# Rows scattered by rank, column-quarter loads turned by VectorE, and a new order of the shared chunks, in a gated two-layer kernel

## The chip, the cores and the metric

The kernel runs on one core of a Trainium2 chip. The metric is the time of one execution on the device in microseconds. TensorE is called PE here (its weight loads PEld), VectorE DVE, ScalarE ACT, GpSimd POOL and SyncE SP, as in the profile.

## What is computed

2048 tokens of 512 features. Layer 1: a layer norm without weights, then one of four gated units chosen by the token's id (the weights of all three products of a unit are the same 512 x 512 matrix), times a tanh gate, added to x. Layer 2: a layer norm, then a mixture of 16 experts of inner width 352, two per token and at most 256 places each, plus one shared gated unit of the same width that all tokens pass, times a second tanh gate, added.

```python
x = x + tanh(g_xattn[0]) * xattn(layernorm(x), token_ids, ctx, ctx, ctx)
x = x + tanh(g_ffn[0]) * ffn(layernorm(x), ...)
# ffn, cut:
scores = sqrt(softplus(xt @ gate_w.T)); _, idx = top_k(scores + gate_b, 2)
buf = zeros((16, 256, 512)).at[e, posc].add(x_pairs)      # dispatch by rank in expert
h = silu(buf @ W1.T) * (buf @ W3.T); out = h @ W2.T       # per expert, width 352
shared = (silu(xt @ Ws1.T) * (xt @ Ws3.T)) @ Ws2.T
return y + shared
```

All of it is float32. Matrix products are made of three products of a high part and a low part of each operand (`product`, L1441): ACT copies the high part out, DVE subtracts it to get the low part, and PE multiplies high by high, high by low and low by high.

## The kernel before, in words

Each engine has its own program in one block; the order of the work is written out by hand, and semaphores (`wait_ge`, `then_inc`) tie the programs together. There is no planner.

**Stage 1** (`step(t, par, known)` on each engine, 19 tiles `t` of 128 rows). Tokens are sorted by their unit, and each unit's group is filled up to whole tiles, so there are NT = 19 tiles for 16 tiles' worth of tokens. POOL gathers a tile's rows of x twice (`gather_xa` for the norm, `gather_xb` for the residual), PE transposes them and multiplies, DVE adds the residual (L1038), ACT writes the normalised rows into the right half of `xh_sb` (L687), and two things leave: POOL scatters both halves, 4 KB a row, to `out` by token (`scatter`, L470), and SP writes the right half, in tile order, to a DRAM tensor `padded` (L405). `xh_sb` has two buffers; DVE's residual of tile t waits until both writes of tile t-2 have landed (L1035, L1036).

**The shared unit.** `rank_gather(j)` on POOL (L481) gathers 128 rows of `padded`, skipping the fill, so that 16 row tiles `j` of ranked tokens come about; four make a block, block b = j // 4. Each row tile lies in `row_tile(j)` (L212), is transposed by PE in four 128 x 128 pieces (`transpose4`, L1447) into a PSUM bank `row_bank(j)`, copied to `bl[b]` by ACT (`transposed`, L706) and subtracted by DVE (`transposed`, L1191). Tiles 0 to 3 pass inside stage 1. Then come the chunks: (b, c) is 128 of the shared unit's columns c for block b, made of two half-chunks (`half_up(n, m)`, L1558, 12 matmuls each, gate side and up side), followed by `silu` and `high` on ACT, `gate` and `low` on DVE. Their order is the list `SEQ` (L1793):

```python
SEQ = [(0, 2), (0, 0), (1, 2), (2, 2), (3, 2), (0, 1)] + [(b, c) for b in range(1, NB) for c in range(2)]
```

Column chunk 2 also carries the 16 router logits. For each block, ACT copies the bank (`copy_logits`), PE transposes it (`logits_of`, L1580), DVE takes 16 of the 128 columns (`take_logits`, L1225), POOL scatters them by token (`send_logits`, L494), and once all four blocks are sent SP loads them back (L427). DVE then routes (L1251 on), with `router(1)` to `router(3)` on ACT between `rows(0)` to `rows(3)`, the copies of the shared unit's output `down(j)` (L1590) out of two PSUM banks; `down(j)` waits for the copy of `down(j-2)`.

**Stage 3** (`stage3`): the 16 experts. POOL gathers an expert's two tiles (`gather`, L543), PE transposes them with the same `transpose4` (`gathered`, L1651), and PE, ACT and DVE go through the unit much as above; POOL adds the results into `out`. The weights of all units, shared and experts, are laid out by `side` on the host (L1804), features cut as k * 128 + p: piece k, partition p.

## Time and profile before

Three runs: 473.49, 474.00 and 474.25 us, median 474.0. The profiled execution took 474.28 us, its span 472.2 us; the 2.1 us between them lie around the span.

| engine | busy us | share of the span | instructions |
|---|---|---|---|
| PE (matmuls) | 455.1 | 96% | 2487 |
| PEld (weight loads) | 391.5 | 83% | 2487 |
| DVE | 321.6 | 68% | 723 |
| ACT | 267.4 | 57% | 415 |
| POOL | 215.0 | 46% | 178 |

The span in 40 slices of 11.8 us, busy tenths in each (9 is 90% or more), with the clock that PE was granted:

```
PE   1999999999999999999999999999999999999995
DVE  6698988978875654479559776676656765676442
POOL 2704445554443465426168345434425445442543
PEclk9999999999999999999999999999999999999999
DMA  7524776887654542254288988899878988888364
```

The shares are averages over stages. A matmul's recorded duration is longer than the distance to the next one, because matmuls are pipelined; the pace is read from stretches of many. Row numbers such as L1449 are lines of the kernel; a line can be that of a helper that several callers share.

### The profile page before, as it was taken

The page shows a single profiled execution, that of the slowest core. Times are in us where ns is not written, and L with a number is a line of the kernel's source. Part 1 is how long each engine was busy: PE and PEld are TensorE (multiplying, and loading weights), DVE is VectorE, ACT ScalarE, POOL GpSimd, SP SyncE. Part 2 cuts the span into 40 slices and gives each one's busy share as a digit, 9 for nine tenths or more (in the row PEclk, how much of TensorE's full clock was granted, in tenths as well). Part 3 has the DMA queues.
Part 4 walks back from the last instruction along what each step waited for, and adds up shares of the span by engine and source line. Part 5 has one row for each costly group of instructions (what it writes and reads, how often), then busy time and mean ns, then how long its engine had stood idle before and what let it go on. Part 6 is the DMA issues. An engine that isn't in the chain of part 4 may idle for free.

```text
span 472.2 us, 7825 instructions
## 1 busy us (share of the span) xinstructions
PE 455.1 (96%) x2487; PEld 391.5 (83%) x2487; DVE 321.6 (68%) x723; ACT 267.4 (57%) x415; POOL 215.0 (46%) x178
## 2 busy tenths in 40 slices
PE   1999999999999999999999999999999999999995
PEld 1677888888888788888888999999999999999994
DVE  6698988978875654479559776676656765676442
ACT  4656666666654643633345675656555766656441
POOL 2704445554443465426168345434425445442543
PEclk9999999999999999999999999999999999999999
DMA  7524776887654542254288988899878988888364
GB/s 305 183 92 127 270 241 202 276 300 239 220 203 165 167 142 98 52 68 56 35 223 166 304 290 270 267 285 272 261 195 258 266 271 257 257 273 244 49 127 92
DMA packets 30476, 95.28 MB, mean 202 GB/s; under 512 B 4976, under 2 KB 7024, under 8 KB 29936
## 3 DMA queue, kind: packets, MB, share of 16 engines
q0 software_dynamic: 17056, 43.92, 37.1%
q1 hardware_dynamic: 13104, 50.98, 31.3%
q8 instruction: 16, 0.26, 0.2%
q14 instruction: 12, 0.10, 0.1%
q10 hardware_dynamic: 288, 0.01, 0.0%
HBM read 67.77 MB, written 28.70 MB: 204 GB/s over the span
## 4 chain that ended last, share of the span: by engine, by line
PE 89%; DVE 4%; DMA 3%; ACT 2%; issue 1%; POOL 0%; POOLq 0%; SPq 0%; DVEq 0%; ACTq 0%
PE psG L1444 47%; PE psY L1444 30%; PE psT L1449 6%; DMA raw<-in_ctx_t 2%; PE psG L1474 1%; PE psG L1707 1%; DMA front<-padded,idxc 1%; PE psG L1524 1%; DVE arena L915 0%; DVE xh_sb L1038 0%; DMA padded<-xh_sb 0%; DVE arena L1054 0%; ACT arena L614 0%; DVE stats L1021 0%; DVE gu L1060 0%
## 5 line engine op out<-in xcount | busy, mean ns | idle before, releaser
L1444 PE MATMUL psY<-arena 128*128 (+1 forms) x366 | 89.3, 395 | 0.6 <-DVE arena L1050 0.6
L1444 PEld LDWEIGHTS psY<-arena 128*128 128x128 f32 x366 | 67.7, 188 | 14.9 <-issue 1.1
L548 POOL DMA_INDIRECT ht<-out,idx x32 | 33.6, 1049 | 64.9 <-PE psT L1449 49.1
L1444 PE MATMUL psY<-slot,arena 128*128 128x512 f32 x240 | 59.1, 395 | 0.0
L1188 DVE TENSOR_TENSOR slot<-raw,slot 128x1536 fp32r<-128x1536 f32 x25 | 43.9, 1758 | 21.0 <-ACT slot L704 20.9
L1444 PE MATMUL psG<-arena 128*128 x216 | 53.9, 399 | 0.0
L1188 DVE TENSOR_TENSOR arena<-raw,arena 128x1536 fp32r<-128x1536 f32 x24 | 42.0, 1758 | 17.4 <-ACT arena L704 17.4
L1444 PEld LDWEIGHTS psY<-slot,arena 128*128 128x128 f32 x240 | 44.3, 188 | 9.3 <-ACT xh_sb L748 0.3
L1444 PE MATMUL psG<-arena,slot 128*128 128x512 f32 x216 | 51.4, 393 | 0.0
L1444 PEld LDWEIGHTS psG<-arena,slot 128*128 128x128 f32 x216 | 40.1, 188 | 8.2
L557 POOL DMA_INDIRECT out<-ys,idx x16 | 31.8, 1986 | 30.5 <-ACT ys L808 21.9
L1444 PEld LDWEIGHTS psG<-arena 128*128 128x128 f32 x216 | 39.3, 188 | 7.5
L1444 PE MATMUL psG<-bl,slot 128*128 128x256 f32 (+1 forms) x264 | 42.1, 314 | 0.0
L475 POOL DMA_INDIRECT out<-xh_sb,idx x19 | 19.6, 1033 | 49.0 <-ACT xh_sb L687 48.3
L818 ACT ACTIVATE s_sb<-psG 128x224 f32<-128x224 f32 (+1 forms) x42 | 15.3, 365 | 46.3 <-PE psG L1444 46.3
L1444 PE MATMUL psG<-slot,bl 128*128 128x448 f32 x192 | 40.6, 366 | 0.0
L1444 PE MATMUL psG<-arena,bl 128*128 128x448 f32 x192 | 40.3, 366 | 0.0
L534 POOL DMA_INDIRECT out<-xh_sb,idxc x16 | 28.2, 1764 | 26.1 <-ACT xh_sb L748 24.3
L1444 PEld LDWEIGHTS psG<-bl,slot 128*128 128x128 f32 x264 | 37.3, 189 | 2.9
L557 POOL DMA_INDIRECT out<-xb,idx x14 | 27.0, 1926 | 26.2 <-issue 15.8
L1444 PEld LDWEIGHTS psG<-arena,bl 128*128 128x128 f32 x192 | 36.1, 188 | 3.3
L1444 PEld LDWEIGHTS psG<-slot,bl 128*128 128x128 f32 x192 | 36.0, 188 | 3.3
(250 smaller groups left out, 820.1 us busy)
## 6 DMA issues: line engine op xcount, KB each, us to landing
raw<-in_w SPq DMA_DIRECT2D x48, 768.0 KB, 5.5
padded<-xh_sb SPq DMA_DIRECT2D x19, 256.0 KB, 2.1
raw<-in_w SPq DMA_DIRECT2D x12, 192.0 KB, 3.1
raw<-in_ctx_t SPq DMA_DIRECT2D x2, 1024.0 KB, 9.0
ht<-in_ctx_t SPq DMA_DIRECT2D x1, 1024.0 KB, 12.1
xh_sb<-in_ctx_t SPq DMA_DIRECT2D x1, 1024.0 KB, 6.1
out<-log_sb SPq DMA_DIRECT2D x4, 256.0 KB, 3.0
ht<-out,idx POOLq DMA_INDIRECT x33, 4.3
```

Source lines behind the costliest of these rows:

```text
L475: pool.indirect_dma_start(out, rows_of(t, 1), xh_sb[:, t % 2, :], None, bounds_check=TOK - 1, oob_is_err=False).then_inc(xh_sent[t % 2], 16)
L534: pool.indirect_dma_start(halves_of_out, ranked(1, j), y2[j % 4], None, compute_op=ALU.add).then_inc(y2_sent[j % 4], 16)
L548: pool.indirect_dma_start(ht[:, n, :], None, halves_of_out, slots(e * NA + a, 0)).then_inc(g_here[n], 16)
L557: pool.indirect_dma_start(halves_of_out, slots(e * NA + a, 1), y3[e % 2][:, a, :], None, compute_op=ALU.add).then_inc(added[a], 16)
L818: act.activation(dst, src, ACT.Silu).then_inc(silu3, 1)
L1188: dve.tensor_tensor(piece(SLOT[r][1], c), raw[:, c, :], as_f32(piece(SLOT[r][0], c)), ALU.subtract).then_inc(w_lo[c], 1)
L1444: ins = pe.matmul(ps, left[a], right[b], start=n == 0 and m == 0, stop=n == total - 1 and m == 2)
L1449: ins = pe.transpose(ps[:, k * P:(k + 1) * P], src[:, k * P:(k + 1) * P], ident)
L1474: pe.matmul(psG[i][:, :], as_f32(minus[:, :]), ctx_raw(e)[:, s], start=True, stop=False)
L1524: ins = pe.matmul(psG[0][:, :], hT[a][:, k * P:(k + 1) * P], ctx(0, k)[b], start=m == 0 and k == 0, stop=m == 2 and k == KD - 1)
L1707: ins = pe.transpose(psG[3][:, o:o + P], gu[:, s:s + P], ident)
```

## The change

Nine edits, in the order of the work:

- `padded` and the SP writes to it go. POOL scatters the normalised half of each of the 19 tiles by rank into a DRAM tensor `by_rank` of 2048 rows, fill rows being out of bounds and left out. The ranks are made by five small POOL operations (`rank_rows`); DVE's `rank_rows` goes.
- SP loads the 16 row tiles from `by_rank` (`load_rows`), in place of POOL's `rank_gather`.
- Tiles 0 to 9 are loaded whole and transposed by PE. Tiles 10 to 15 are loaded in four DMAs each, one per quarter of the columns, so that the four groups of 32 partitions hold the four quarters; DVE then turns the tile in 32 x 32 blocks straight into the PSUM bank (`turn`).
- Features are cut as p * 4 + k: the host lays W1, W3 and the router's weights out so, and PE's transposes of row tiles, those of the experts too, read every fourth column (`transpose4_rows`). `turn` reads with the same step.
- `SEQ` has block 0's chunk 1 ahead of block 2's chunk 2.
- PE, ACT and DVE follow the new list, with the transposes spread between the chunks. DVE's order after stage 1 is (a bare number is the subtraction of that tile): `take_logits(0)`, 6, 7, `gate(1)`, `low(1)`, 8, `turn(10)`, 9, `turn(11)`, `gate(2)`, `low(2)`, `take_logits(1)`, 10, `turn(12)`, 11, `turn(13)`, `gate(3)`, 12, `turn(14)`, `low(3)`, 13, `turn(15)`, 14, 15, `gate(4)`, `low(4)`, `take_logits(2)`, `gate(5)`, `take_logits(3)`, `low(5)`, `split(0, 2, 0)`.
- DVE subtracts the low part of the shared unit's down weights (`split(0, 2, 0)`) after `low(5)` instead of before `take_logits(3)`.
- `logits_of` transposes 16 rows of `log_sb` instead of 128.
- The waits on `padded_sent` become waits on `ranked_sent`.

```diff
+        def quarters(ap):
+            return ap.rearrange("p (b i k) -> p k b i", b=KD, k=KD)
...
+            def load_rows(j):
+                all_landed(sp, ranked_sent, j + E1 - 1)
...
+                rows = by_rank[j * P:(j + 1) * P, :]
+                if j < TURN_ROWS:
+                    sp.dma_start(row_tile(j), rows).then_inc(ht_here[j % 8], 16)
+                else:
+                    for q in range(KD):
+                        sp.dma_start(row_tile(j)[q * QP:(q + 1) * QP, :].rearrange("t (b d) -> t b d", b=KD),
+                                     rows[:, q * P:(q + 1) * P].rearrange("(b t) d -> t b d", b=KD)).then_inc(ht_here[j % 8], 16)
...
-                sp.dma_start(padded[t * P:(t + 1) * P, :], xh_sb[:, t % 2, D:2 * D]).then_inc(padded_sent[t % 2], 16)
...
+                if 6 <= t < 6 + TB:
+                    load_rows(t - 6)
+                elif t >= 11 and t - 7 < 3 * TB - 1:
+                    load_rows(t - 7)
+            for j in range(3 * TB - 1, NJ):
+                load_rows(j)
...
+                pool.indirect_dma_start(by_rank, bass.IndirectOffsetOnAxis(ap=rank_of[:, t:t + 1], axis=0),
+                                        xh_sb[:, t % 2, D:2 * D], None,
+                                        bounds_check=TOK - 1, oob_is_err=False).then_inc(ranked_sent[t % 2], 16)
...
+            AHEAD = {2: (8, 9), 3: (10, 11), 4: (14, 15)}
+            BETWEEN = {1: (6, 7), 3: (12,)}
+            for n in range(1, 6):
+                for j in AHEAD.get(n, ()):
+                    transposed(j)
                 silu(n)
                 if SEQ[n][1] == 2:
                     copy_logits(n)
+                for j in BETWEEN.get(n, ()):
+                    transposed(j)
                 high(n)
+                if n == 3:
+                    transposed(13)
+                elif n == 4:
+                    split(0, 2, 0)
...
+            def turn(j):
+                dve.wait_ge(ht_here[j % 8], 16 + 16 * KD)
+                dve.wait_ge(bT_ps, j)
+                dve.wait_ge(bT_lo, j - 1)
+                dve.transpose(row_bank(j), quarters(row_tile(j))).then_inc(bT_ps, 1)
...
+            def transpose4_rows(ps, src):
+                for k in range(KD):
+                    ins = pe.transpose(ps[:, k * P:(k + 1) * P], src.rearrange("p (i k) -> p k i", k=KD)[:, k], ident)
...
-                transpose4(row_bank(j), row_tile(j)).then_inc(bT_ps, 1)
+                transpose4_rows(row_bank(j), row_tile(j)).then_inc(bT_ps, 1)
...
-                    t = pe.transpose(psY[1][:, s], log_sb[:, s], ident)
+                    r = slice(LOG0, LOG0 + E2)
+                    t = pe.transpose(psY[1][:, j * P + LOG0:j * P + LOG0 + E2], log_sb[r, s], ident[r, r])
...
+            for n in range(1, 6):
+                if n == 1:
+                    transposed(4)
+                    transposed(5)
                 half_up(n, 0)
+                if n == 1:
+                    logits_of(0)
+                if n < 3:
+                    transposed(2 * n + 4)
+                    transposed(2 * n + 5)
                 half_up(n, 1)
+                if n > 1 and SEQ[n][1] == 2:
+                    logits_of(SEQ[n][0])
...
-                    transpose4(psT[a], ht[:, n, :]).then_inc(g_ps, 1)
+                    transpose4_rows(psT[a], ht[:, n, :]).then_inc(g_ps, 1)
...
-SEQ = [(0, 2), (0, 0), (1, 2), (2, 2), (3, 2), (0, 1)] + [(b, c) for b in range(1, NB) for c in range(2)]
+SEQ = [(0, 2), (0, 0), (1, 2), (0, 1), (2, 2), (3, 2)] + [(b, c) for b in range(1, NB) for c in range(2)]
...
-        t[:, :, :, :I_MLP] = w.reshape(e, I_MLP, KD, P).transpose(0, 3, 2, 1)
+        t[:, :, :, :I_MLP] = w.reshape(e, I_MLP, P, KD).transpose(0, 2, 3, 1)
```

## Rows read from the trace of the kernel before

**Rows 1.** Busy us by stretch, with (x) instructions, granted clock, DMA share, GB/s.
```profile
60.00:151.70 91.70, 91.70 (x476) 76.67 (x475) 75.60 (x264) 56.35 (x101) 44.77 (x46) 1.00 0.68 231
151.70:193.00 41.30, 40.76 (x211) 33.72 (x210) 19.64 (x39) 18.91 (x33) 22.56 (x24) 1.00 0.39 131
...
244.00:449.00 205.00, 205.00 (x1226) 187.10 (x1225) 135.15 (x175) 126.91 (x181) 93.44 (x61) 1.00 0.86 247
```

**Rows 2.** Chain that ended last, shared stretch: start us, us, what.
```profile
157.78 2.01 DMA padded<-xh_sb
159.89 4.48 DMA front<-padded,idxc
...
192.88 8.37 PE psY L1444 x36
```

**Rows 3.** Instructions in order of time, logits to `rows(1)`: start us, us, engine, line.
```profile
186.03 0.22 DVE L1228 COPY ranked_logits<-psY 128x64 f32<-128x64 f32 x1
...
190.82 0.97 POOL L498 DMA_INDIRECT logit_rows<-ranked_logits,idxc  x1 [0.30 <-issue]
...
195.07 0.43 DVE L1251 SCALAR_TENSOR_TENSOR big<-logits 128x256 f32<-128x256 f32 x1 [5.46 <-DMA logits<-logit_rows]
...
196.78 1.28 ACT L774 ACT_TABLE_LOAD   x1
...
198.18 0.67 ACT L748 ACTIVATE xh_sb<-psY,tg 128x512 f32<-128x512 f32 x1
```

**Rows 4.** Chain that ended last: tile transposes, a half-chunk, logit transposes.
```profile
78.08 0.87 PE psT L1449 x8
78.95 2.74 PE psG L1444 x12
...
171.49 0.44 PE psY L1587 x4
```

**Rows 5.** Groups by line: count, busy us, mean ns of one, idle before.
```profile
L1449 PEld LDWEIGHTS psT<-cst,ht 128*128 128x128 f32 x160 | 18.1, 141 | 0.4
L1474 PE MATMUL psG<-raw,minus 128*128 128x512 f32 x12 | 8.3, 783 | 0.3 <-ACT arena L614 0.3
L1195 DVE TENSOR_TENSOR arena<-psT,arena 128x512 fp32r<-128x512 f32 x12 | 7.7, 685 | 5.4 <-ACT arena L708 5.4
L708 ACT ACTIVATE arena<-psT 128x512 fp32r<-128x512 f32 x12 | 6.5, 593 | 0.0
```

**Rows 6.** Single DVE lines, ns min/median/max: L1284 steps 64 B, L1318 8 B.
```profile
L1254 DVE TENSOR_SCALAR big<-big x1: 289/289/289, 196.0 to 196.0; 128x256 f32<-128x256 f32 x1
L1275 DVE TENSOR_TENSOR big<-big,small x2: 424/424/424, 203.6 to 206.3; 128x256 f32<-128x256 f32 x2
L1284 DVE TENSOR_TENSOR big<-big x1: 603/603/603, 210.1 to 210.1; 128x256 f32<-128x256 f32 x1
L1315 DVE TENSOR_TENSOR small<-psT,small x1: 191/191/191, 232.8 to 232.8; 128x32 f32<-128x32 f32 x1
L1318 DVE SCALAR_TENSOR_TENSOR idx<-small x1: 192/192/192, 233.4 to 233.4; 128x32 int32<-128x32 f32 x1
```

**Rows 7.** POOL and SP: order of time, L475's landing us, L405's issue ns, one wait.
```profile
90.79 1.01 POOL L475 DMA_INDIRECT out<-xh_sb,idx  x1 [1.55 <-ACT xh_sb L687]
...
92.10 0.97 POOL L491 DMA_INDIRECT ht<-padded,idxc  x1 [0.30 <-DMA padded<-xh_sb]
...
97.13 0.75 DVE L1038 SCALAR_TENSOR_TENSOR xh_sb<-psY,tg,xb 128x512 f32<-128x512 f32 x1 [0.63 <-PE psY L1444]
...
158.58 1.01 POOL L475 DMA_INDIRECT out<-xh_sb,idx  x1 [5.32 <-ACT xh_sb L687]
...
DMA to landing us min/median/max: 2.7/3.8/5.0
...
L405 SPq DMA_DIRECT2D padded<-xh_sb x19: 319/320/327, 41.3 to 157.8; - x19
...
POOL xb L468 <- DVE xh_sb L1038: 11.7, 2, 11.2
```

More of the change, by code:

```diff
@@ L34 @@
 KD = D // P
+QP = P // KD
 NJ = TOK // P
@@ L246, in gated_layer @@
         r2_whot, r2_wsrc, r2_w = (sem(f"r2_{n}") for n in ("whot", "wsrc", "w"))
-        rank_hot, rank_src, rank_idx, rows_idx = (sem(n) for n in ("rank_hot", "rank_src", "rank_idx", "rows_idx"))
-        padded_sent = [sem(f"padded_sent{n}") for n in range(2)]
+        rank_hot, rank_src, rank_idx, rows_idx, rank_steps = (
+            sem(n) for n in ("rank_hot", "rank_src", "rank_idx", "rows_idx", "rank_steps"))
+        ranked_sent = [sem(f"ranked_sent{n}") for n in range(2)]
         xa_here = [sem(f"xa_here{n}") for n in range(4)]
@@ L514, in _ @@
             gather_xa(5)
+            rank_rows()
             for t in range(2, LAST):
@@ L520, in _ @@
                 scatter(t - 2)
-                if SPLIT <= t < SPLIT + TB:
-                    rank_gather(t - SPLIT)
-                if ROWS0 < t <= ROWS0 + 2 * TB - 1:
-                    rank_gather(t - ROWS0 + TB - 1)
-            rank_gather(3 * TB - 1)
-            for j in range(3 * TB, NJ):
-                rank_gather(j)
             for b in range(NB):
@@ L754, in _ @@
             stage1(act, step)
-            for n in range(1, 5):
-                if 1 < n < NB:
-                    transposed(n * TB)
-                    transposed(n * TB + 1)
+            AHEAD = {2: (8, 9), 3: (10, 11), 4: (14, 15)}
[3 more added lines that the diff above has]
+                    transposed(j)
                 silu(n)
@@ L1035, in residual @@
                         dve.wait_ge(xh_sent[par], landed(t - 4, par))
-                        dve.wait_ge(padded_sent[par], landed(t - 4, par))
+                        dve.wait_ge(ranked_sent[par], landed(t - 4, par))
                     c = (t - 2) % 4
@@ L1136, in step @@
                     rank_digits(known - 3)
-                if known in (5, 6):
-                    rank_rows(known - 5)
                 if known == 7:
@@ L1230, in _ @@
             stage1(dve, step)
-            for n in range(1, 5):
-                if 1 < n < NB:
-                    transposed(n * TB)
-                    transposed(n * TB + 1)
-                if SEQ[n - 1][1] == 2:
-                    take_logits(SEQ[n - 1][0])
-                if n < NB:
-                    transposed(n * TB + 2)
-                    transposed(n * TB + 3)
-                gate(n)
-                low(n)
+            take_logits(0)
+            transposed(6)
+            transposed(7)
+            gate(1)
+            low(1)
+            transposed(8)
+            turn(10)
+            transposed(9)
+            turn(11)
+            gate(2)
+            low(2)
+            take_logits(1)
+            transposed(10)
+            turn(12)
+            transposed(11)
+            turn(13)
+            gate(3)
+            transposed(12)
+            turn(14)
+            low(3)
+            transposed(13)
+            turn(15)
+            transposed(14)
+            transposed(15)
+            gate(4)
+            low(4)
+            take_logits(2)
+            gate(5)
+            take_logits(3)
+            low(5)
             split(0, 2, 0)
-            take_logits(3)
-            hidden(5)
             B = [x_[:, :, :] for x_ in big]
@@ L1617, in _ @@
             stage1(pe, step)
-            for n in range(1, NB):
-                transposed(n * TB)
-                transposed(n * TB + 1)
+            for n in range(1, 6):
+                if n == 1:
+                    transposed(4)
+                    transposed(5)
                 half_up(n, 0)
-                if SEQ[n - 1][1] == 2:
-                    logits_of(SEQ[n - 1][0])
-                transposed(n * TB + 2)
-                transposed(n * TB + 3)
-                half_up(n, 1)
-            half_up(4, 0)
-            logits_of(2)
-            half_up(4, 1)
-            half_up(5, 0)
-            logits_of(3)
-            half_up(5, 1)
+                if n == 1:
[3 more added lines that the diff above has]
+                    transposed(2 * n + 5)
+                half_up(n, 1)
+                if n > 1 and SEQ[n][1] == 2:
+                    logits_of(SEQ[n][0])
             up(6)
@@ L1819 @@
     w3 = side(np.concatenate([f["L0_ffn_Ws3"][None], f["L0_ffn_W3"]]))
-    w1[0, :, :, I_MLP:I_MLP + E2] = f["L0_ffn_gate_w"].reshape(E2, KD, P).transpose(2, 1, 0)
+    w1[0, :, :, I_MLP:I_MLP + E2] = f["L0_ffn_gate_w"].reshape(E2, P, KD).transpose(1, 2, 0)
     arrays = {
```

66 lines of the change are left out of this document (32 added, 34 removed).

## The prediction

> **What bounds the kernel now.** I read the busy time by stretches first. From 60.0 to 151.7 us, and again from 244.0 to 449.0, TensorE (PE) is busy for the whole stretch, always at a granted clock of 1.00, the higher of its two levels (2.4 GHz) [rows 1]. In those stretches the time is the sum of what PE is given. Only the shared stretch from 151.7 to 193.0 has holes, 0.54 us of them, and the start and the last 20 us. The chain of waits then says what ends late in the shared stretch: the last normalised tile, its write to `padded`, a gather back of 4.48 us, and from there PE alone [rows 2]. The order of time shows a second chain beside it, which no share shows: the router logits of block 3 are taken by VectorE (DVE) at 186.03, sent by four indirect DMAs of GpSimd (POOL), reloaded, and reach DVE at 195.07; ScalarE (ACT) runs `router(1)`, `high(6)` and a table load in order, and only then copies the rows of `down(1)` out at 198.18 to 198.85 [rows 3]. `down(3)` needs that bank. The four `down` of 9 matmuls take 8.37 us [rows 2] where 36 times 227 ns, a half-chunk's pace (12 in 2.74, [rows 4]), would be 8.17, so this chain already holds PE up by 0.2 us. Work taken off PE ahead of it is worth nothing beyond what also brings the logits sooner.
>
> **The change part by part.**
>
> *PE loses tile transposes.* Eight take 0.87 us in a stream, 109 ns each [rows 4]. Tiles 10 to 15 lose 6 x 4 x 0.109 = 2.6 us.
>
> *PE's logit transposes become narrow.* 16 of them, now 0.44 us per four [rows 4]. The labels name the moving operand first (`minus` was the stationary one in L1474, `raw` the moving one), so in a transpose the data are the weight load [rows 5]. The data keep 128 columns and only the identity shrinks from 128 to 16. I bound the saving by 0 (the load sets the pace) and by all of it, 1.7 us, and take 0.05 per transpose, 0.8 in all, most of it ahead of block 3's logits. The Trainium skill, "TensorE: Matmul & The Clock Gate", section "LDWEIGHTS (loading the stationary operand)", says a load's time follows its columns and that 32 x 128 takes as long as 128 x 128; by it the saving would be nil, and no row of before shows a 16-row load.
>
> *DVE gets six turns.* No such operation is in the trace. The bounds: a one-input operation on 256 columns takes 0.29 us [rows 6], twice that is 0.58; two inputs on 512 columns take 0.68 (L1195, [rows 5]); and a step of 64 B (L1284 writes every 16th float, L1275 steps over none) costs 0.18 us per 256 elements (0.60 against 0.42, [rows 6]), which on 512 elements gives 0.68 + 0.36 = 1.04. I take 0.69, nearest to the 512-column row. That puts 6 x 0.69 = 4.1 us on DVE, while its subtraction per tile (0.68) and ACT's copy (0.59) stay [rows 5].
>
> *SyncE (SP) loads instead of POOL gathers.* 10 single loads and 6 x 4 quarter loads, 0.32 us each to issue [rows 7]: 1.3 us for a turned tile, landing 2.0 us later as `padded`'s write does [rows 2]. The latest, tile 15: last normalised tile at 157.8 [rows 2]; POOL's `out` scatter 158.58 to 159.59; ranked scatter from 159.9, landed 3.8 later (the scatter's median, [rows 7]) at 163.7; four loads, 167.0. DVE turns that tile only at about 176.6, so 9 us cover it. Behind these loads on SP stand the loads of expert 1, which wait for the last tile's transpose, some 4 us later than now; ACT splits them only after `up(9)`, tens of us later, so that is covered. The loads inside SP's loop wait only for scatters one or more tiles old, so the weight slices behind them start on time.
>
> *POOL in stage 1.* One scatter more per tile, at 1.01 us and 0.3 to the next, stands where a rank gather stood in most tiles [rows 7]. The reuse of `xh_sb` now also waits for the ranked scatter: from 92.10 landed at 95.9, wanted at 97.13 [rows 7]; 1.2 us to spare. Cost nothing; if it lands after the longest 5.0 us, the cover is just gone. The five index operations of `rank_rows` on POOL lie in front of `xb`'s gather, which waited 11.2 us at most [rows 7]: nothing. DVE's four small `rank_rows` operations go, at no gain, since PE has no hole there.
>
> *The shared stretch in its new order.* I lay it out with a tile transpose at 0.44, a half-chunk of 12 matmuls at 2.74 [rows 4], DVE 0.69 (subtraction 0.66), ACT 0.6, 0.2 us from PE to another engine and 0.05 to 0.12 otherwise. The old order, laid out so, ends `down(3)` at 201.3, as the trace does (201.24). The new one: tiles 6 and 7 are subtracted at 160.6, so `half_up(2,0)` starts at 160.7 (PE idle 1.3); tiles 8 and 9 transposed by 164.3; DVE is then nearly unbroken: tiles 8 to 11 with turns 10 and 11, `gate(2)`, turns 12 and 13, ready at 171.8, before PE wants block 2 at 172.9, since block 0's second chunk fills 167.5 to 172.9. Tiles 12 to 15 are ready at 178.6, and `logits_of(2)` waits until 179.2 for ACT's copy, which stands behind tile 15 (PE idle 0.8). `half_up(5,1)` ends at 185.1, the logits at 185.5, and `take_logits(3)` at 186.2 against 186.65 in the old order laid out the same way. `down(0)` starts 1.9 us sooner, but `rows(1)` ends at 198.7 against 199.2 and `down(3)` at 200.9 against 201.3: a gain of 0.4. The layout runs late at tile 7 (160.57 where the trace has 160.04), which is worth another 0.25 net of a similar lateness in the old order, and the narrower logits 0.35. Sum: -1.0 us. Of 2.6 us taken off PE, 1.6 turn into a longer wait at `down(3)`.
>
> After that DVE's routing starts by the same amount sooner, and what PE waits for next (the counts of `r2_tot`) comes out of that routing, so the gain is carried to the end.
>
> *PE's remaining transposes read with a step.* 10 tiles of the shared part and 16 x 2 of the experts, 168 transposes, now load every fourth float. Bounds: nothing, and DVE's price, 0.70 ns per element (603 - 424 over 256) x 128 = 90 ns each. For nothing speak the step of 8 B, which costs DVE nothing (0.19 both, [rows 6]), and that PE itself takes in 512 moving columns in 227 ns, twice the rate per column of a transpose (109 for 128). I take nothing, the nearer row being PE's own; the other end is the first rival.
>
> The profiled execution took 474.28, its span 472.2. Less 1.0 that is 473.3; the median of the runs is 0.28 below the profiled one, so 473.0.
>
> **Rivals.**
>
> *The step costs PE (slower).* DVE's rows at 64 B show that a step can cost; if 16 B is dear already, each of 42 tiles takes 0.36 us more. Stage 3 has no hole: 32 x 0.36 = 11.5; four tiles in stage 1, 1.4; the shared stretch with both prices ends 1.6 late instead of 1.0 early in my layout. 474.0 + 11.5 + 1.4 + 1.6 = 488.5; with a doubled pace (109 more) 491. It decides as soon as a step costs more than 8 ns per transpose (128 of them undo the 1.0). The Trainium skill, "Advanced Engine Details and Errata", section "Memory Cachelines", speaks for it: SBUF lines are 16 bytes and an access wants two hits per line, while a step of four floats has one; the 64 B rows agree, the 8 B row too, and no row has 16 B.
>
> *The turn is dear, PE not.* At 1.04 the layout gives +1.1 - 0.6 = +0.5, 474.5; at 1.25, above the bound, +1.7, 475.7. It decides from some 1.12.
>
> *The logits chain has slack that I don't see.* Then all 2.6 us come through: 471.4. Against it: the 0.2 us at `down(3)`.
>
> *The ranked scatter lands late.* From 5 us on DVE's residual waits; 0.5 us over in 14 tiles would be 7 us, 481. The landing rows (2.7 to 5.0) hardly reach it.
>
> **How the numbers follow.** Within 0.2% (0.95 us) no measurement of this kernel can be told from no change. No price on PE, turn between 0.58 and 1.04: 0.50, its own range 471.8 to 475.0; of it 0.27 faster, 0.18 the same, 0.05 slower. Step costs PE: 0.37, all slower. Dear turn: 0.04, slower. Slack in the chain: 0.06, faster. Late scatter: 0.03. Sum: faster 0.33, same 0.18, slower 0.49. The cases of both signs are far apart, and the range has to reach into the second: 471.0 to 490.5 leaves out about 0.15.
>
> **What would show it.** Weight loads of L1449's successor at 141 ns and eight transposes still in 0.87 us: no price on PE; The turn's duration is read directly. PE's wait at the last `down` of block 0 should grow to about 1.7 us. Eight expert transposes in 1.5 us or more would make the prediction wrong by 11 us and more; `take_logits(3)` before 184 would make it too cautious.

## The result, and the profile after

The changed kernel took 477.74 us (median of 5 runs, 476.65 to 478.97) beside 473.49 for the kernel before (5 runs): 1.0085 times as long, interval 1.0069 to 1.0102. It is slower by some 4 us, where 1.0 us faster was forecast. The profiled execution, the fastest of the five, took 476.65, its span 474.8.

Four rows of the chain of waits cut the span into comparable stretches (start, duration, what): the last product of stage 1 (called A below), the first `down` of block 1 (B), an expert's `down` (D) and the last expert's (E). First the kernel before, then after.

```profile
149.00 2.74 PE psY L1444 x12
212.25 8.28 PE psY L1444 x36
274.93 4.12 PE psY L1444 x18
...
433.23 8.21 PE psY L1444 x36
```

```profile
148.49 2.72 PE psY L1487 x12
213.76 8.28 PE psY L1487 x36
275.25 0.97 PE psT L1499 x8
276.65 4.11 PE psY L1487 x18
...
435.85 8.19 PE psY L1487 x36
```

A to B, the shared unit, went from 63.25 to 65.27: +2.02. B to D went from 62.68 to 62.89, D to E, twelve experts, from 158.30 to 159.20: together +1.11 in stage 3 and just ahead of it. A itself comes 0.51 sooner: in this execution stage 1's first steady product starts 0.93 earlier (41.74 for 42.67), and from there to A 106.33 became 106.75. These add up to the 2.6 us between the two spans. With the same start the parts would add up to 3.55; the 4.25 between the medians are 0.7 more. That is less than executions of one kernel differ by here (1.2 us among the five of before, 2.3 among the five of the changed kernel), and no trace shows what it is.

What sets B is the moment at which the router logits of all blocks reach DVE. Before, that is 46.07 us after A, and B follows 17.18 later [rows 3]; in the changed kernel it is 48.09 after A, and B again follows 17.18 later. The 2.02 us are therefore the logits' delay, whole. Half of it, 1.02, lies ahead of `take_logits(3)` (186.54 here; 37.03 after A before, 38.05 now), the other half between it and the logits' arrival (9.04 before, 10.04 now):

```profile
186.54 0.22 DVE L1254 COPY ranked_logits<-psY 128x64 f32<-128x64 f32 x1
```

```profile
192.10 2.46 DMA logit_rows<-ranked_logits,idxc
194.57 1.99 DMA logits<-logit_rows
```

The busy time by stretches, as in [rows 1] (length, then PE, PEld, DVE, ACT, POOL, the granted clock, DMA):

```profile
60.00:151.70 91.70, 91.70 (x478) 77.18 (x477) 74.72 (x260) 56.02 (x101) 50.02 (x50) 1.00 0.68 225
151.70:193.00 41.30, 38.95 (x186) 31.19 (x186) 25.01 (x45) 19.12 (x33) 19.15 (x19) 1.00 0.40 132
244.00:449.00 205.00, 205.00 (x1212) 187.22 (x1211) 133.84 (x174) 126.91 (x181) 91.60 (x61) 1.00 0.87 248
```

PE's holes between 151.7 and 193.0 have grown from 0.54 us to 2.35. Stage 3 still has none, so its extra microsecond is more work, not a wait. PE's timeline names the holes (in brackets: idle before, and what ended it):

```profile
159.59 3.04 PE L1487 MATMUL psG<-arena,slot 128*128 128x512 f32 x12 [0.44 <-DVE arena L1221]
179.72 0.42 PE L1638 MATMUL psY<-cst,log_sb 16*128 16x16 f32 x4 [1.91 <-ACT log_sb L756]
200.41 2.34 PE L1487 MATMUL psY<-slot,arena 128*128 128x512 f32 x9 [2.44 <-ACT xh_sb L778]
```

The last is `down(3)`, the wait that was forecast to grow to 1.7. The second was forecast as 0.8: `logits_of(2)` waits for ACT's copy, which stands behind tile 15. The new operations themselves (count, then busy, mean ns; the two turns whose tile lies in `front` have a row of their own, 1103 ns):

```profile
L1215 DVE STREAM_TRANSPOSE psT<-ht 128x512 f32<-128x512 f32 x4 | 4.4, 1100 | 0.5
...
L1499 PEld LDWEIGHTS psT<-cst,ht 128*128 128x128 f32 x144 | 18.9, 209 | 0.2
L1492 PEld LDWEIGHTS psT<-cst,front 128*128 128x128 f32 x76 | 8.8, 141 | 1.3 <-DVE front L1100 0.5 <-issue 0.4
L1638 PEld LDWEIGHTS psY<-cst,log_sb 16*128 16x128 f32 x16 | 1.3, 136 | 3.4 <-ACT log_sb L756 2.3 <-issue 1.1
```

A turn takes 1.10 us. A stepped weight load takes 209 ns where an unstepped one in the same kernel takes 141, but the pace of the transposes, which the chain shows, went only from 8 in 0.87 [rows 4] to 8 in 0.97. A logits load of 16 rows takes 136 ns, nearly as long as one of 128 rows before (138), and four transposes take 0.42.

### The profile page after: what moved, and what is told of

Read it like the earlier page. It is cut to its first block, busy times and chain, and to the rows that moved or that the text cites. A ratio compares the mean times of both kernels' runs of the same rounds, so it can differ in the third digit from the quotient of the medians.

```text
span 474.8 us, 7825 instructions
## 1 busy us (share of the span) xinstructions
PE 453.7 (96%) x2463; PEld 390.0 (82%) x2463; DVE 326.0 (69%) x725; ACT 268.3 (57%) x415; POOL 221.3 (47%) x186
## 4 chain that ended last, share of the span: by engine, by line
PE 86%; DVE 5%; issue 2%; POOL 2%; ACT 2%; DMA 2%; POOLq 0%; DVEq 0%; ACTq 0%
PE psG L1487 45%; PE psY L1487 29%; PE psT L1499 4%; PE psT L1492 3%; POOL logit_rows L535 2%; PE psG L1756 1%; PE psG L1524 1%; DMA tok_i<-in_ids 1%; PE psG L1574 1%; DMA logit_rows<-ranked_logits,idxc 1%; DVE arena L947 0%; DVE psT L1215 0%; DVE big L988 0%; DVE gu L1232 0%; DMA logits<-logit_rows 0%
## 5 line engine op out<-in xcount | busy, mean ns | idle before, releaser
L1207 DVE TENSOR_TENSOR slot<-raw,slot 128x1536 fp32r<-128x1536 f32 x25 | 43.9, 1760 | 20.7 <-ACT slot L734 20.6
L1207 DVE TENSOR_TENSOR arena<-raw,arena 128x1536 fp32r<-128x1536 f32 x24 | 42.0, 1757 | 17.5 <-ACT arena L734 17.5
```

Of the source, the lines that this page charges most:

```text
L1207: dve.tensor_tensor(piece(SLOT[r][1], c), raw[:, c, :], as_f32(piece(SLOT[r][0], c)), ALU.subtract).then_inc(w_lo[c], 1)
```

## The experiments

Each kernel was timed beside the kernel before. "Ratio" is to it, with its interval; the other columns are from one profiled execution of each, in us: A to B, the time from A to the logits' arrival at DVE, and D to E. "Fall" says whether TensorE's granted clock fell inside A to B there.

| kernel | ratio | A to B | A to logits | fall | D to E |
|---|---|---|---|---|---|
| before | 1 | 63.25 | 46.07 | no | 158.30 |
| changed | 1.0085 (1.0069 to 1.0102) | 65.27 | 48.09 | no | 159.20 |
| e3 before, step on TensorE | 1.0038 (1.0023 to 1.0053) | 63.65 | 46.47 | no | 159.52 |
| e4 before, scatter by rank | 0.9988 (0.9977 to 0.9999) | 62.74 | 45.52 | no | 158.16 |
| e1 plain turn | 1.0053 (1.0034 to 1.0072) | 65.22 | 46.43 | yes | 159.21 |
| e5 plain turn twice | 1.0148 (1.0119 to 1.0177) | 67.02 | 49.80 | no | 159.21 |
| e6 step in shared unit only | 1.0077 (1.0050 to 1.0103) | 66.64 | 47.94 | yes | 158.14 |
| e2 step of 2 | 1.0157 (1.0134 to 1.0180) | 67.96 | 50.78 | yes | 158.97 |
| e7 no step | 1.0031 (1.0017 to 1.0044) | 65.13 | 46.34 | yes | 158.19 |
| e9 step in writing | 1.0061 (1.0040 to 1.0083) | 63.72 | 46.54 | no | 158.14 |
| e8 logits copy first | 1.0071 (1.0052 to 1.0091) | 66.10 | 47.30 | yes | 159.20 |
| e17 e9, logits copy first | 1.0019 (1.0004 to 1.0034) | 62.88 | 45.70 | no | 158.14 |
| e10 split early | 1.0098 (1.0073 to 1.0122) | 65.70 | 48.52 | no | 159.20 |
| e12 hole filled | 1.0076 (1.0051 to 1.0101) | 66.61 | 49.42 | yes | 159.19 |
| e13 down(3) late | 1.0097 (1.0078 to 1.0117) | 64.86 | 47.82 | behind B | 159.20 |
| e16 before, split late | 1.0020 (1.0011 to 1.0030) | 64.15 | 46.97 | no | 158.30 |
| e14 four turns | 1.0004 (0.9995 to 1.0014) | 62.51 | 45.31 | no | 158.16 |
| e18 e14, split late | 1.0033 (1.0021 to 1.0045) | 63.49 | 46.31 | no | 158.14 |
| e15 two turns | 0.9990 (0.9979 to 1.0000) | 61.89 | 44.62 | no | 158.17 |
| e19 two turns apart | 1.0014 (1.0002 to 1.0027) | 62.58 | 45.39 | no | 158.16 |

From the logits' arrival to B it is 17.2 to 17.3 us in every row but five. In e1, e6, e7 and e8 the clock fell between the two, and it is 18.7 to 18.8; in e13, where `down(3)` was moved behind other products, it is 17.0. So whatever moves A to B here moves the logits, or is a fall of the clock, worth 1.5 to 1.6 us there. In e1, e5 and e7 tiles 10 to 15 pass the shared unit and the router with their features in another order, so the numbers, and the experts chosen, are others; D to E is within 0.05 us of that of the kernels with the same transposes.

**The parts alone: e3 and e4.** The theory was that the step of 4 floats costs both engines and the rest little; the rival, that GpSimd's new path or the new order is to blame.

```diff
-  transpose4(...)   # tiles of the shared unit and of the experts; weights k * 128 + p
+  transpose4_rows(...)   # the same, every fourth float; weights p * 4 + k
```

> The kernel before, with one edit: TensorE's transposes of the shared unit's and of the experts' tiles read every fourth float, and the weights of the up products are laid out to fit. No turn on VectorE, no scatter by rank, the order of before. Theory A (the step costs TensorE 12 ns on each transpose, as the changed kernel's 8 in 0.97 us against 0.87 say): stage 3 is longer by 1.0 to 1.2 us, stage 1 and the shared unit by 0.2 to 0.6, the time 1.2 to 1.8 us above before, about 475.0. Rival B (stage 3 of the changed kernel is longer for another reason, and the step is covered by the products before it): within 0.4 us of before, 473.1 to 473.9.

D to E is 1.22 longer, 12.7 ns for each of its 96 transposes, A to B 0.40, the time 0.38%, 1.8 us. Theory A holds: stage 3 has no hole to hide even 12 ns.

```diff
-  padded, rank_gather
+  by_rank, load_rows(j) whole for all 16 tiles; TensorE turns them; order, logits and weights of before
```

> The kernel before, with one part of the change: the rows are scattered by rank by GpSimd and loaded plainly by SyncE for all of tiles 0 to 15, which TensorE turns as before; the order of before, contiguous transposes, logits transposed from 128 rows. Theory A (the new path costs stage 1 a stall where the second scatter holds the row buffer, and nothing behind it): stage 1 is longer by 0.3 to 1.0 us, the shared unit and stage 3 the same within 0.2, the time 0.3 to 1.0 above before, about 474.1. Rival B (the new path also feeds the shared unit late): the shared unit alone is longer by over 1 us, and the time over 1.5 us above before.

Both theories expected a loss; it is the one part that seems to gain, 0.6 us, with an interval that just leaves out none. Stage 1 is longer (106.83 for 106.33), as theory A had it: in the changed kernel too DVE's residual waits there for the ranked scatter (waited for: total, times, longest):

```profile
DVE xh_sb L1070 <- DMA by_rank<-xh_sb,rank_of: 0.9, 2, 0.5
```

But the last gather of 4.48 us and the wait behind it [rows 2] are gone from the shared unit, and the logits come 0.55 sooner.

**The turn: e1, e5.**

```diff
-  quarters: "p (b i k) -> p k b i"
+  quarters: "p (k b i) -> p k b i"
```

> The changed kernel, with one edit: VectorE's turn of tiles 10 to 15 reads consecutive floats instead of every fourth (the features of these tiles come out in another order, so their numbers in the shared unit are others; every instruction stays). Theory A (VectorE's step of 4 floats makes the turn 1.10 us and with that tiles 12 to 15, logits(2) and logits(3) late): the turn takes 0.60 to 0.75 us, six of them give back about 2.4 us of VectorE, the stretch from the first chunk of the shared unit to the end of down(3), 51.5 us in the changed kernel, goes to 49.0 to 50.0, and the time is 1.6 to 2.4 us below the changed kernel, about 475.6. Rival B (the chain is late by its order and by GpSimd's sends, whatever a turn takes): the stretch stays above 51.0 and the time within 0.5 us of the changed kernel's 477.7.

The turn takes 0.727 us. `take_logits(3)` comes 1.45 us sooner after A (36.60 for 38.05), and `down(3)` starts 50.26 after A instead of 51.92: theory A. The time fell by a third of a per cent, 1.5 us (1.6 to 2.4 were expected), but A to B only from 65.27 to 65.22, for in this execution something else came in. PE's hole before `down(3)`, 2.23 us here, is followed by this (columns as above; the clock is the third number from the end):

```profile
200.00:201.00 1.00, 1.00 (x5) 0.80 (x4) 0.93 (x3) 0.98 (x2) 1.00 (x1) 0.77 0.00 0
201.00:202.00 1.00, 1.00 (x4) 0.81 (x3) 0.93 (x3) 0.58 (x1) 0.69 (x2) 0.50 0.55 33
202.00:203.00 1.00, 1.00 (x4) 0.71 (x4) 0.67 (x2) 0.26 (x1) 1.00 (x1) 0.50 0.73 94
203.00:204.00 1.00, 1.00 (x4) 0.81 (x3) 0.78 (x2) 0.98 (x3) 0.22 (x1) 0.52 1.07 156
204.00:205.00 1.00, 1.00 (x6) 0.83 (x5) 0.92 (x3) 1.00 (x1) 0.99 (x1) 1.00 0.89 84
```

After the hole the granted clock is 0.50, 1.2 GHz, for some 3.4 us, then 2.4 GHz again: 4 matmuls a microsecond for 5 or 6. The changed kernel's profiled execution had the same hole and no fall. Of its five executions the two slowest, 478.97 and 478.54, had a mean granted clock of 0.996 and 0.993; the median one, 477.74, had 0.998, as the profiled one, so a fall explains the slow end of its times and not its median. e6's at 0.993 to 0.995 took 477.65 to 479.06 and its one at 0.999 475.02.

```diff
+  dve.transpose(xb[:, 0, :], quarters(row_tile(j)))   # ahead of each turn, read by nobody
```

> As the kernel with the plain turn, but each of the six turns is done a second time, into a tile that nobody reads: two of 0.65 to 0.7 us in place of one. Theory A: with 1.3 to 1.4 us for each tile VectorE is the bound from tile 12 on, about five of the six added turns stand in the chain to logits(3), and the time is 2.5 to 4 us above the kernel with one plain turn, above the changed kernel's by 1 to 2. Rival B: within 0.5 us of the kernel with one plain turn.

+4.1 us against e1. A to B is 67.02 without a fall, 3.3 more than with turns of 0.727 and no fall (e9, below): of the 4.2 us of added turns most stand on the path. Theory A in kind; the time is 3.0 above the changed kernel's, not 1 to 2, and five of its six executions have a clock of 0.987 to 0.994, so falls are part of it.

**The step: e6, e2, e7, e9.**

```diff
-  transpose4_rows(psT[a], ht[:, n, :])   # experts
+  transpose4(psT[a], ht[:, n, :])        # and their weights k * 128 + p
```

> The changed kernel, with one edit: the tiles of the experts are transposed from consecutive floats, their weights laid out as before; the step stays in the shared unit. Theory A (TensorE pays the step in stage 3, where it has no hole: 104 to 128 transposes by 10 to 12 ns): stage 3 is 1.0 to 1.3 us shorter, the shared stretch as in the changed kernel, the time 1.0 to 1.5 us below it, about 476.5. Rival B (stage 3 is longer by its gathers or its clock): no change within 0.4 us.

D to E came back to 158.14, as theory A said. The time doesn't show it: the intervals of the two overlap, and five of e6's six executions have a clock of 0.995 or less.

```diff
-  feature 4 p + k; four loads of a turned tile
+  feature 256 h + 2 p + s, k = (h, s); eight loads
```

> The changed kernel with a step of 2 floats (8 bytes) in place of 4, for TensorE's transposes and VectorE's turns alike, the weights laid out to fit, and eight loads of a turned tile instead of four. The Trainium skill, Advanced Engine Details and Errata, section Memory Cachelines, wants two hits in a line of 16 bytes, which a step of 8 bytes has: by it the turn would take 0.73 us, as with consecutive floats, and a transpose on TensorE 109 ns. Rival: the price grows with the step, and half of it is left: 0.9 us and 115 ns. By the first the time is that of the kernel with the plain turn less what TensorE's step costs, 1.4 to 3 us below the changed kernel; by the second 1 to 1.5 below. If SyncE's eight loads, 3.5 us for a tile, land after VectorE wants the tile, the turns of tiles 14 and 15 start later and less of this is seen.

VectorE and TensorE part here:

```profile
L1216 DVE STREAM_TRANSPOSE psT<-ht 128x512 f32<-128x512 f32 x4 | 2.9, 727 | 3.2 <-DMA ht<-by_rank 3.0
```

```profile
L1500 PEld LDWEIGHTS psT<-cst,ht 128*128 128x128 f32 x144 | 18.8, 207 | 0.2
```

At 8 bytes the turn costs what consecutive floats cost, as the rule of two hits of the Trainium skill, Advanced Engine Details and Errata, section Memory Cachelines, has it; the weight load is as slow as at 16 bytes, against it, and eight transposes take 0.96, not 0.87. The rival, half of each price, fell too. The loads became the wait (3.0 us of the turns' idle time), so the time says nothing.

```diff
-  quarters: "p (b i k) -> p k b i"; transpose4_rows; weights p * 4 + k
+  quarters: "p (k b i) -> p k b i"; transpose4; weights k * 128 + p
```

> The kernel with the plain turn, and TensorE's transposes too read consecutive floats, with the weights of before (tiles 10 to 15 have their features in another order in the shared unit). What is left of the change is the scatter by rank, the turns on VectorE at 0.73 us, the narrow logits and the new order. Theory A (the parts add up: scatter -0.6, TensorE's step 1.8 taken away, the rest +1.3): 0.3 to 1.2 us above before, about 474.9. Rival B (without any step the change gives what it saves on TensorE): below before by 0.5 us or more.

+0.31%, 1.5 us, a little above theory A's 0.3 to 1.2: no step is left and the change is still slow. Its trace has the fall, after a hole of 2.24.

```diff
-  dve.transpose(row_bank(j), quarters(...))     # block b: tokens 32 b + t
+  dve.transpose(row_bank(j) as "p (k t b) -> p k b t", quarters(...))   # block b: tokens 4 t + b
```

> The changed kernel without any step on the reading side, and with the right numbers: a turned tile is loaded so that a block of 32 partitions holds tokens 4t+b in runs of 32 features, VectorE reads consecutive floats and writes every fourth one into the bank, and TensorE and the weights are as before. Theory A (the price is in reading SBUF with a step): the turn takes 0.73 us, eight transposes 0.87, and the time is that of the kernel with no step at all, about 475.9. Rival B (the step costs on the writing side as well): the turn takes 1.1 us or more, the shared stretch is as long as in the changed kernel, and the time is 1 to 1.2 us below the changed kernel, by TensorE's contiguous transposes alone, about 476.6.

The turn takes 0.727 with every fourth float written, and a transpose on TensorE what it took before (D to E 158.14): theory A on the price. The time, +0.61%, 2.9 us, was to be that of e7 (+0.31%); the intervals still touch, and the clock had a part: two executions at a clock of 0.998 and 0.999 took 475.40 and 474.90, four at 0.994 to 0.996 took 476.26 to 477.57. A to B is 63.72, so the two steps cost the shared stretch 1.55, nearly all of it the turns' (e1 and e7 differ in TensorE's step alone, and `take_logits(3)` by 0.09). `take_logits(3)` stands 36.51 after A, 0.52 sooner than before, and still the logits come 0.47 later. The other 0.98 over e4, with six tiles fewer on TensorE, belongs to the rest together: the new order, the six turns at 0.727, and what now runs beside the sends (e10, below).

**The order: e8, e17, e10.**

```diff
-  ACT: 14, 15, silu(4), copy_logits(4), high(4)     DVE: 14, 15, gate(4), low(4), take_logits(2)
+  ACT: silu(4), copy_logits(4), 14, 15, high(4)     DVE: 14, 15, take_logits(2), gate(4), low(4)
```

> The changed kernel, with ScalarE's silu(4) and logits copy of block 2 ahead of its copies of tiles 14 and 15, and VectorE's take_logits(2) ahead of gate(4). Theory A (GpSimd's four sends of block 2 begin so late that they hold those of block 3): take_logits(2) comes 1.5 to 2 us sooner, block 3's sends start within 0.4 us of take_logits(3), the last wait before down(3) shrinks by about 1, and the time is 0.8 to 1.3 us below the changed kernel. Rival B (the chain hangs on take_logits(3) alone): take_logits(3), its sends and the time stay within 0.4 us.

`down(3)` starts 51.13 after A (51.92 in the changed kernel), but the theory's mechanism fell: block 3's sends start 0.97 after `take_logits(3)` here, in the changed kernel and (0.98) in the kernel before, held by nothing in any of them. What went is `logits_of(2)`'s 1.91 us (1.3 are left, for tile 15). The time can't be told from the changed kernel's.

> The new order with turns that read consecutive floats (the kernel that writes with a step), and with ScalarE's logits copy of block 2 ahead of its copies of tiles 14 and 15 and VectorE's take_logits(2) ahead of gate(4). Theory A (block 2's sends hold block 3's): block 3's sends start within 0.4 us of take_logits(3) plus the 0.98 of the trace of before, the hole before down(3) is 0.6 to 1.0 shorter, the time 0.5 to 1.5 us below that kernel's 476.4. Rival B (as the kernel that made only this edit to the changed kernel showed, the split beside the sends gives the gain back): within 0.4 us.

With turns of 0.73 the same edit takes 0.84 out of A to B, most of what e9 lost to e4, and 0.4% off the time, 2.0 us and so more than theory A's 1.5; block 3's sends start 0.97 after `take_logits(3)`, as in e8, so the reason is e8's. Fewer of its executions have a low clock (3 of 11 at 0.995 or less).

The other half of the logits' delay lies in the sends. Before, all four of block 3 take 0.97; in the changed kernel the first two are longer, 0.77 us together, and DVE is at work beside them (`low(5)`, L1237, then the split, L1207):

```profile
187.51 1.34 POOL L535 DMA_INDIRECT logit_rows<-ranked_logits,idxc  x1 [0.44 <-issue]
189.15 1.37 POOL L535 DMA_INDIRECT logit_rows<-ranked_logits,idxc  x1 [0.30 <-issue]
190.82 0.97 POOL L535 DMA_INDIRECT logit_rows<-ranked_logits,idxc  x1 [0.30 <-issue]
```

```profile
187.32 0.69 DVE L1237 TENSOR_TENSOR arena<-gu,arena 128x512 fp32r<-128x512 f32 x1 [0.56 <-ACT arena L765]
187.93 1.75 DVE L1207 TENSOR_TENSOR slot<-raw,slot 128x1536 fp32r<-128x1536 f32 x1
```

```diff
-  gate(5), take_logits(3), low(5), split(0, 2, 0)
+  split(0, 2, 0), gate(5), take_logits(3), low(5)
```

> The changed kernel with VectorE's split(0,2,0) ahead of gate(5) and take_logits(3), in a gap of VectorE of 4 us, instead of behind them. Theory A (the first two sends of block 3 take 1.34 and 1.37 us instead of 0.97 because the split, 1.75 us on VectorE, runs beside them): all sends take 0.97, the logits land 0.7 us sooner, TensorE's hole before down(3) shrinks from 2.4 to 1.7, the time is 0.6 to 0.9 below the changed kernel, and more where a shorter hole no longer lets the clock fall. Rival B (two sends are long for another reason): they stay at 1.3, and the time within 0.3.

Neither: the split now met block 2's first send, and that took 2.39 us. Block 2's last send, far from the split, took 1.32 beside `low(5)`:

```profile
183.43 1.76 DVE L1207 TENSOR_TENSOR slot<-raw,slot 128x1536 fp32r<-128x1536 f32 x1 [0.55 <-ACT slot L734]
...
188.67 0.69 DVE L1237 TENSOR_TENSOR arena<-gu,arena 128x512 fp32r<-128x512 f32 x1 [0.56 <-ACT arena L765]
```

```profile
183.64 2.39 POOL L535 DMA_INDIRECT logit_rows<-ranked_logits,idxc  x1 [7.13 <-DVE ranked_logits L1254]
...
188.88 1.32 POOL L535 DMA_INDIRECT logit_rows<-ranked_logits,idxc  x1 [0.30 <-issue]
```

So the split is not the only cause. In all 20 traces a send of logits that begins while DVE subtracts two operands that both lie in SBUF (the split and `low` do) is longer by what is left of the subtraction, less some 0.13 us: 1.42 with 1.55 left and 0.35 with 0.48 left here; in the changed kernel 0.37 with 0.50 left of `low(5)` for the first send and 0.40 with 0.53 left of the split for the second. A send that begins ahead of the subtraction is not longer, as e16 shows, where the last one starts 0.03 us before the split:

```profile
189.53 0.96 POOL L498 DMA_INDIRECT logit_rows<-ranked_logits,idxc  x1 [0.30 <-issue]
```

```profile
189.56 1.76 DVE L1188 TENSOR_TENSOR slot<-raw,slot 128x1536 fp32r<-128x1536 f32 x1
```

Nor is one beside a DVE operation that takes an operand from PSUM: in the changed kernel the send at 186.10 began with 0.52 us of `gate(5)` left and took 0.97. The Trainium skill, SBUF — State Buffer, section Who interferes with whom, says that a VectorE instruction with two SBUF inputs contends with a GpSimd instruction that reads SBUF; the split and `low` have two, and the rows agree.

With block 2's sends this late, block 3's began 1.6 us after the moment at which `take_logits(3)` would have let them, and the logits came no sooner (48.52 after A). In the trace of before the split lies in a gap between two blocks' sends, and `low(5)` begins 0.63 us into a send; the change moved both.

**The holes: e12, e13.**

```diff
+  9 x pe.matmul(psT[1], ...)   # ahead of down(3)
```

> The changed kernel with nine matmuls more (2.04 us, into a bank that nobody reads) between down(2) and down(3), where TensorE has its hole of 2.44 us. Theory A (after a hole of over 2 us the granted clock falls to 0.50 for some 3.3 us in most executions, as in the traces of four of these kernels from 200 us on, and costs 1.7): the granted clock of the core stays at 0.997 or more in every run, the runs lie closer together, and the median falls by 0.8 to 1.7 us, to about 476.4. Rival B (the clock falls for another reason, or its fall costs nothing here): runs at 0.993 to 0.995 remain, and the median stays within 0.4 us.

Four of six executions took 476.28 to 476.92 at 0.997 or more, two 479.2 to 479.4 at 0.993 to 0.994. The profiled one is of the latter: no fall at the filled hole, but one after the other hole, the 1.93 us before `logits_of(2)` (0.70 and 0.50 in 180 to 184). So theory A is half right, since there were two holes. All traces together say the same. From 45 to 460 us, eight of the twenty have no hole over 0.9 us on TensorE, and none of them a fall; twelve have one of 1.9 to 3.2 us, and in seven of these the clock falls once, within 1.2 us of the end of such a hole. What decides between the seven and the five, no run shows.

```diff
-  down(0) to down(3), up(7)
+  down(0) to down(2), up(7), down(3)
```

> The changed kernel with up(7) ahead of down(3) on TensorE: 5.5 us of products stand where TensorE waited 2.44 us for the logits chain. Theory A (that wait is where the work taken off TensorE went): no hole before down(3), the shared stretch 2.2 to 2.5 us shorter, no fall of the clock, the time 2.4 to 4 us below the changed kernel, 474 to 475. Rival B (the logits chain ends last anyway: what VectorE makes of the logits holds TensorE at r2_tot, just behind): the wait moves there, and the time stays within 0.6 us of the changed kernel.

Rival B. The hole before `down(3)` is gone, and PE waits nearly as long, 2.1 us, at `r2_tot` (waited for: total, times, longest):

```profile
PE psT L1689 <- DVE small L1331: 2.1, 1, 2.1
```

The logits chain runs on through VectorE's routing and holds PE at its end; moving `down(3)` only moves the wait.

**The versions that came out: e16, e14, e18, e15, e19.**

```diff
-  split(0, 2, 0), take_logits(3), hidden(5)
+  take_logits(3), hidden(5), split(0, 2, 0)
```

> The kernel before, with one edit: VectorE's split(0,2,0) behind hidden(5) instead of ahead of take_logits(3). Theory A (TensorE is the bound there, and the logits have at most 0.2 us to give): take_logits(3) comes 1 us sooner, and the time is 0 to 0.3 us below before. Rival B (the split now runs beside the sends, or down(0) waits for it): 0.3 us or more above before.

Rival B, by another queue: `take_logits(3)` came 1.3 us sooner, the logits 0.8 later. SP's load of weights waits for the split and now goes out just ahead of the logits' load:

```profile
191.34 0.33 SPq L387 DMA_DIRECT2D raw<-in_w  x1
191.72 0.43 SPq L427 DMA_DIRECT2D logits<-logit_rows  x1
```

That load goes out 1.2 us sooner than before, but takes 4.14 us to land instead of 2.1:

```profile
191.72 4.14 DMA logits<-logit_rows
```

The logits reach DVE at 195.88, not 195.07.

```diff
   e4, with turns as in e9, logits_of on 16 rows, and
+  DVE, after the subtraction of tile j: turn(j + 2), for tiles 12 to 15
```

> The order of before, rows scattered by rank and loaded plainly, logits transposed from 16 rows, and only tiles 12 to 15 turned by VectorE, from consecutive floats into a bank written with a step, so that TensorE and all weights are as before. Theory A (the new order and the step made the change slow, not the turn as such): TensorE loses 16 transposes, 1.74 us, all ahead of the last logits; the shared stretch is 1.4 to 1.9 us shorter than with the scatter by rank alone, and the time is 1.5 to 2.5 us below before, about 471.7. Rival B (VectorE's four turns hold its gates, or GpSimd's sends the logits): the stretch is shorter by 0.5 at most, the time that of the scatter alone, 0.6 below before.

A to B only 0.23 under e4: PE waits 0.22 and 0.73 for VectorE at blocks 2 and 3 (`DVE arena L1219`). Rival B.

> As the kernel with four turns, with VectorE's split(0,2,0) behind hidden(5) instead of ahead of take_logits(3). In the trace of before the split ends at the moment at which take_logits(3) begins, 1.2 us after the last logits stood in the bank. Theory A: take_logits(3) comes 1 us sooner, the split meets only the last send, any hole before down(3) is gone, and the time is up to 0.5 us below the kernel with four turns. Rival B (the split then runs beside two sends and stretches them by 0.4 us each, or TensorE is the bound): within 0.2 us, or above.

Rival B in the time, but as in e16 and not by stretched sends: only the last is longer, 1.17, and the logits' load takes 4.11 us to land.

```diff
-  turns of tiles 12 to 15
+  e15: of 14 and 15      e19: of 12 and 14, with 13 and 15 on TensorE
```

> As the kernel with four turns and the order of before, but only tiles 14 and 15 turned by VectorE. Theory A (VectorE's load between block 2 and block 3 decides): TensorE loses 0.87 us and waits at most 0.3 for block 3; the shared stretch is 0.4 to 0.9 shorter than with the scatter by rank alone (62.7), the time 1.0 to 1.5 us below before, about 472.7. Rival B (any turn holds the gates or block 3 as long as it saves): stretch 62.5 or more, time 0.1 to 0.6 below before.

> As above, with tiles 12 and 14 turned by VectorE and 13 and 15 by TensorE, so that one turn stands between block 2's gate and block 3's instead of two. Theory A: TensorE does not wait for block 3 at all, the shared stretch is 0.7 to 0.95 shorter than with the scatter by rank alone, the time 1.2 to 1.5 us below before, about 472.5. Rival B: as above.

e15 has theory A's stretch, 61.89, 0.85 under e4, with no hole in the shared unit, and the best trace (span 470.6); over its runs it is 0.1% below before, 0.5 us, not the 1.0 to 1.5 of theory A, and this measurement hardly tells it from none. In e19 PE waits 0.27 and 0.32 at tiles 13 and 15, and the gain is gone. Nothing tried beats before by more than e4 and e15 do, 0.1% each.

## Why the prediction was wrong

What bounds the shared stretch was read rightly: the chain of the router logits. The 2.6 us taken off TensorE came back, and more, as waits: 2.44 us at `down(3)`, on this chain, and 1.91 at `logits_of(2)`, behind the turns. Three terms of the sum were wrong: the turn's price, TensorE's step, and what two moved subtractions do to the sends, which the sum leaves out. By the prediction's steps:

- **DVE gets six turns.** This is the step that failed first: 0.69 taken, 1.10 measured, above the bound of 1.04 that was to be the worst. The bound had the price of a step of 64 bytes in writing; 16 bytes in reading cost as much. 0.727 without a step shows that the nearest row was well chosen for the turn itself. The step alone brings `take_logits(3)` 1.45 us later (e1 against the changed kernel).
- **The shared stretch in its new order.** With a plain turn `take_logits(3)` came as the layout said: 0.52 sooner than before (e9), forecast 0.45. In part that was luck, for the scatter by rank alone, with every transpose on TensorE, gives 0.67 (36.36 after A in e4): the turns and the order added nothing to it. And behind it stand the sends. `gate(5)` moved ahead of `take_logits(3)`, so that `low(5)` follows at once, and the split moved behind both; this is in the change's list, and the sum has no line for it. So `low(5)` and the split meet the first two sends, 0.37 and 0.40 us, and the gain of 0.52 comes out as logits that are 0.47 later.
- **PE's remaining transposes read with a step.** Taken as nothing, measured 12 ns each: 1.1 us from D to E (159.20, and 158.14 without, e6), and in the order of before 0.4 in the shared unit (e3). The rival "the step costs PE" was to decide from 8 ns on, and had 90: it came in by its own threshold and at an eighth of its price. Both ends were weighed, the small price between them was not.
- **PE's logit transposes become narrow.** 0.05 each taken, under 0.01 measured; the load, 136 ns for 138, did not shrink.
- **POOL in stage 1.** Costed at nothing, 0.4 to 0.5 measured; the 1.2 us to spare were used up in two tiles. **SyncE's loads** held: a quarter load took 0.43 us to issue, not 0.32, but no turn waited for one in the changed kernel.
- **The gain is carried to the end.** The loss was, and with it holes of 2 us, after which the clock fell in part of the executions. e9 and e7, alike but for the turn's write and its loads, have A to B of 63.72 without a fall and 65.13 with one. No step spoke of this.

Put together, A to B: -0.52 by scatter, order and plain turns, +0.09 by TensorE's step and +1.45 by the turns' step, all at `take_logits(3)`, then +0.77 by the sends and +0.23 in the landings make the 2.02. Behind B the 1.1 is TensorE's step.

The rival "the turn is dear" had the mechanism of the shared stretch, at 0.04, with 475.7 at most; it was to decide from 1.12, which 1.10 just misses. The chances had slower ahead, 0.49, but most of that on TensorE's step at 488.5. The measured 477.74 lies inside the range 471.0 to 490.5 only because the range reached across to that rival; no case came out near it, so that is luck. Open is why the clock falls after such a hole in one execution and not in another, and why stage 1's start differs by up to 1 us between executions.

## What to carry to other kernels

A chain over several engines that already ends level with the busiest one can turn a gain on that engine into a wait, and the wait can cost the clock as well: shorten the chain first. Cost every operation that a reordering moves by what it now runs beside, on its own engine, on an engine that it can hold up (here GpSimd's sends beside a subtraction), and in the queue behind it. Before an access pattern gets a step, price it on each engine that reads it; here the writing side of the turn bore it at no cost.

## What the runs showed of the hardware

- Reading SBUF with a step of 16 bytes takes VectorE's 32 x 32 transpose of 128 x 512 floats from 0.727 to 1.10 us; 8 bytes cost nothing, nor does writing PSUM at every fourth float.
- TensorE's load of a 128 x 128 stationary operand goes from 141 to 207 ns at 8 bytes and 209 at 16; in a stream all but 12 ns of it is hidden.
- An indirect DMA's issue on GpSimd, 0.97 us, that begins while VectorE subtracts two SBUF operands takes longer by what is left of the subtraction, less some 0.13 us (1.34, 1.37 and 2.39 with 0.50, 0.53 and 1.55 left). Begun 0.03 us ahead of it, or beside an operation with an operand in PSUM, it takes 0.96 to 0.99.
- A load of SyncE issued 0.4 us behind a load of weights took 4.1 us to land, not 2.1 (e16, e18).
- TensorE's granted clock fell from 1.00 to 0.50 for some 3.4 us after holes of 1.9 to 3.2 us, in seven of twelve traces with such a hole and in none of eight without.
